# An audio tower on one core: who splits the weights, when batch 1's taps run, and where the last batches' second products and stores stand

## The chip, the cores and the metric

The kernel runs on one core of one Trainium2 chip. The metric is the device time of one execution in microseconds, lower is better. TensorE (PE) does the matmuls, VectorE (DVE), ScalarE (ACT) and GpSimd (POOL) the elementwise work, SyncE (SP) starts the transfers. The engines run side by side, each through its own list of instructions in order, and wait for each other by semaphores.

## What is computed

Eight batches of 750 frames with 192 features go through one block: a token front end (seven-tap convolution, pointwise product, relu, pooling by two, 2D Fourier transform, norm), an attention over tokens with 12 heads, and a routed feed-forward block. Cut to its steps:

```python
h = conv7_per_feature(x) + b_dw                       # "taps": 7 multiply-adds over 750 frames
h = maxpool2(relu(h @ w_pw + b_pw))                   # 375 tokens of 192
h = layernorm(real(fft2(h))) * gamma + beta           # first norm
w = layernorm(h) @ w_qkv                              # 12 heads of 64
Pi = softmax(sum_d (w / norm_n(w))**2 * temp)         # over the tokens
h = h - (w * Pi / (1 + Pi_norm @ w**2)) @ w_out + b_out
z = layernorm(h); n = layernorm(z) * g1 + b1          # routed block on z
s = sigmoid(n @ Wr + br)                              # the 56 lowest scores get attention
merged = where(lowest, softmax(q k / 4) v @ Wo + bo, (n + s * pooled) @ Wm + bm)
h2 = z + merged
n2 = layernorm(h2) * g2 + b2
out = h + h2 + gelu(n2 @ W1 + bf1) @ W2 + bf2
```

## The kernel before

Tokens lie on 125 partitions by 3 tiles where they are normed, and 192 features on 96 partitions by 2 where they are multiplied. Five weights (w_qkv, W1, Wk, Wv, Wm) are used in two parts: a high part (the weight rounded to fp32r) and a low part (the weight minus the high part), and the tokens likewise, so that a `split_product` is three matmuls.

`pipeline` runs ten steps on every engine: `step(p, q, r, w)`. In step k the front end and token attention of batch p = k run beside the routed block of batch q = k - 1, the feed-forward products of batch r = k - 2 and, on DVE, the taps of batch w = k + 1. Step 0 has only a front (and the taps of batch 1), steps 3 to 6 are a loop, step 8 has no front, and step 9 has only the feed-forward products of batch 7. The taps of batch 0 come ahead of step 0 in three tiles (`depthwise_first`, L376).

The order of each engine is written out by hand in its `step`:

- **POOL** (L776): clears whole tiles, splits w_qkv (L785 to L794: a copy, then a subtraction), then in step 0 the other four weights behind batch 0's norms. Beside that it takes the power of every norm and makes two additions a batch.
- **SP** (L286): loads, then x of batch 1 when batch 0's taps are done (L302), 22 transfers of weights (L306), then W1 into the space in which w_qkv lay (L309) once w_qkv is split; one store a batch (L319).
- **DVE** (L697): in step 0 pools batch 0, then the first norm (L414 on), the token split (L452), taps 0 to 2 of batch 1, head sums (L458 to L464), taps 3 and 4, the maximum of the token logits (L469), the token softmax and products, taps 5 and 6, and the third norm.
- **ACT** (L981): relu, the spectrum's copies (L853 on), sines, token split (L869), squares, exponentials, gelus.
- **PE** (L1318): `forward_up` (L1292) is the first product of the feed-forward block with W1, 6 blocks of 128 columns; `forward_down` (L1306) the second with W2, 3 tiles by 6 blocks, each two matmul instructions. In step 8 the second products of batch 6 stand between the attention steps of batch 7: tile 0 ahead of the last `turn` (a transpose of probabilities), tile 1 in two halves behind `values`, tile 2 in two parts around the output products (`mixed`, `replaced`, L1284). In step 9 all first products stand ahead of all second ones. `forward_down` waits for all six gelus once.

Behind the output products DVE adds them up and norms (`fifth_norm`, `fifth_norm_end`), PE transposes the result n2 (L1046), ACT and DVE split it, and the next first product can start. `result` (L694) adds the second products to the residual in two pieces, and SP stores the batch. The first product writes the same PSUM tile yb as the second, so it waits for the results of the batch before (L1299).

Of the kernel before, what the change touches and what calls it, by code (L numbers as in the profile page):

```python
# [4 lines left out]
B, S, D, K = 8, 750, 192, 7  # L5
# [29 lines left out]
def audio_tower(nc, dram, out):  # L35
# [3 lines left out]
    with ExitStack() as ctx:  # L39
# [112 lines left out]
        w_qkv32 = probsT[0:C].rearrange("c j t q -> c (j t q)")[:, 0:CT * IT * 128].rearrange("c (t i) -> c t i", t=CT)  # L152
        n2 = sb("n2", [P, T, D])
# [23 lines left out]
        split = signal("split")  # L177
# [73 lines left out]
        MEMSETS, WEIGHTS = 5, 5  # L251
        SPLIT = MEMSETS + 2 * WEIGHTS
# [9 lines left out]


# [18 lines left out]
        def first(b):  # L282
            return isinstance(b, int) and b == 0

        @block.sync
        def _(sp):  # L286
# [21 lines left out]
            sp.wait_ge(split.sem, MEMSETS + 2)  # L308
# [20 lines left out]
            for b in range(B - 3, B):  # L329
                store(b)  # L330
            sp.wait_ge(*stored.of(B - 1))

        @block.vector
        def _(dve):
# [41 lines left out]
            def depthwise_first():  # L376

                dve.wait_ge(*x_ready.of(0))
                for t in range(T):
# [3 lines left out]
                    for k in range(K):  # L383
                        for c in range(CT):
# [7 lines left out]
                            ins.then_inc(sem, 1)  # L392

# [295 lines left out]
            def result(b, i):  # L689
# [4 lines left out]
                dve.tensor_tensor(y_out[:, t0:t1, :], yb[0:P, i, 0:D * (t1 - t0)].rearrange("p (t d) -> p t d", d=D),  # L694
                                  res_f[:, t0:t1, :], ALU.add).then_inc(y_done.sem, 1)

            def step(p, q, r, w):  # L697
# [63 lines left out]
                if last:  # L761
                    result(r, 0)
                    result(r, 1)
# [3 lines left out]
                if middle:  # L767
                    forward_input(q)
                if front:
# [6 lines left out]
        def _(pool):  # L776
            pool.memset(half3[:], -0.5).then_inc(consts.sem, 1)
            pool.memset(xhT[:].bitcast(fp32), 0.0).then_inc(split.sem, 1)
            pool.memset(n2T[:].bitcast(fp32), 0.0).then_inc(split.sem, 1)
            pool.memset(nT[:].bitcast(fp32), 0.0).then_inc(split.sem, 1)  # L780
            pool.memset(w_v[:].bitcast(fp32), 0.0).then_inc(split.sem, 1)
            pool.wait_ge(split.sem, 4)
            pool.memset(nT[C:C + 1, 0, 0, :].bitcast(fp32), 1.0).then_inc(split.sem, 1)

            def split_weight(k, parts, weight):  # L785

                high, low = (parts[:, i, ..., 0:weight.shape[-1]] if len(weight.shape) == 3 else parts[:, i] for i in range(2))
                pool.tensor_copy(high, weight).then_inc(split.sem, 1)
                pool.wait_ge(split.sem, MEMSETS + 2 * k + 1)
                pool.tensor_tensor(low, weight, high, ALU.subtract).then_inc(split.sem, 1)  # L790

            pool.wait_ge(consts.sem, FILLS)
            pool.wait_ge(qkv_in.sem, QKV)
            split_weight(0, w_qkv, w_qkv32)  # L794
# [6 lines left out]
            def step(p, q, r, w):  # L801
# [10 lines left out]
                if first(p):  # L812
                    pool.wait_ge(rest_in.sem, REST)
                    pool.wait_ge(w_1_in.sem, 16)
                    split_weight(1, w_1, w_qkv32)
                    split_weight(2, w_k, w_k32)
                    split_weight(3, w_v, w_v32)
                    split_weight(4, w_mp, w_m[:])
# [20 lines left out]
        def _(act):  # L839
# [7 lines left out]

            def spectrum_parts(b):
# [13 lines left out]
            def front_input(b):  # L862
                act.wait_ge(*xhT_ready.of(b))
                if first(b):
                    act.wait_ge(split.sem, MEMSETS)
# [27 lines left out]
            def routed_input(b):  # L893
# [3 lines left out]
                else:  # L897
                    act.wait_ge(split.sem, SPLIT)
# [46 lines left out]
            def exponentials(b, j):  # L945
                act.wait_ge(*qmax_done.of(b, j + 1))
                if j == 0 and first(b):
                    act.wait_ge(split.sem, SPLIT)
# [18 lines left out]
            def forward_input(b):  # L967
                act.wait_ge(*n2T_ready.of(b))
                if first(b):
                    act.wait_ge(split.sem, MEMSETS)  # L970
# [515 lines left out]
```

## Time and profile before

| | |
|---|---|
| three timed runs | 654.84, 647.49, 654.38 us; median 654.38 |
| the profiled execution | 647.86 us |
| its span, first to last instruction | 646.0 us |
| mean granted PE clock over the span | 0.917 of full speed |
| busy share of the span | PE 85%, weight loads 70%, DVE 70%, ACT 36%, POOL 15% |
| chain that ended last, by engine | PE 58%, DVE 23%, ACT 11%, waiting to issue 6% |
| steps 2 to 7 | about 66.5 us each, PE clock at full |

Times in the rows are microseconds from the start of the span. An engine's busy time counts its own instructions, and a transfer's time runs from issue to landing. In the chain of waits each piece is followed back to what released it. A granted clock of 1.00 is 2.4 GHz, 0.50 is 1.2 GHz; where the profile has no record of it, as in the first 33 us, it shows 1.00.

### The profile page before, as it was taken

The numbers are of one execution on the slowest core, as the hardware profiler recorded it, in microseconds if no ns is written. First come the engines' busy times: TensorE is split into PE (matmuls) and PEld (weight loads), VectorE is DVE, ScalarE is ACT, GpSimd is POOL, SyncE is SP. The second block draws the span as 40 slices with busy tenths as digits, with TensorE's granted clock in tenths as the row PEclk, the third lists the DMA queues.
The fourth block names the chain that finished last, engine by engine and source line by source line (L and its number), as shares of the span: only waits on it lengthen the run. The fifth ranks groups of instructions, "written<-read, shape, count | busy, mean of one in ns | idle before, by whom it ended". The sixth has DMA issues, their size and how long they took to land.

```text
span 646.0 us, 9489 instructions
## 1 busy us (share of the span) xinstructions
PE 547.0 (85%) x3344; PEld 449.4 (70%) x3344; DVE 450.1 (70%) x1234; ACT 231.0 (36%) x614; POOL 94.4 (15%) x76
## 2 busy tenths in 40 slices
PE   1447398979999999999999999999989998787976
PEld 1326176758777878777877787788768777775765
DVE  5738868576878887789778887788778564824130
ACT  0014113440357035712581158125721564124311
POOL 5318010100210021002100301030103010200010
PEclk9987589576999999999999999999999999959689
DMA  8240010010000000010001000100000000000000
GB/s 209 75 124 1 0 36 2 1 36 1 1 1 24 15 19 1 2 36 18 0 0 36 18 0 0 36 18 0 0 0 19 2 0 1 19 0 2 1 18 18
DMA packets 8212, 12.73 MB, mean 20 GB/s; under 512 B 1891, under 2 KB 6717, under 8 KB 8184
## 3 DMA queue, kind: packets, MB, share of 16 engines
q1 hardware_dynamic: 8184, 12.37, 7.2%
q8 instruction: 16, 0.26, 0.2%
q14 instruction: 12, 0.10, 0.1%
HBM read 10.07 MB, written 2.30 MB: 19 GB/s over the span
## 4 chain that ended last, share of the span: by engine, by line
PE 58%; DVE 23%; ACT 11%; issue 6%; DMA 1%; POOL 1%; DVEq 0%; ACTq 0%; SPq 0%
PE xb L1138 8%; PE yb L1054 8%; PE zb L1054 7%; PE yb L1314 7%; PE xb L1084 5%; ACT probs L952 3%; PE xb L1093 3%; ACT w_sq L879 2%; DVE dw L390 2%; DVE nr L541 2%; PE zb L1284 2%; ACT w_s L878 2%; DVE st L343 2%; PE zb L1211 2%; ACT probsT L957 2%
## 5 line engine op out<-in xcount | busy, mean ns | idle before, releaser
L799 POOL TENSOR_TENSOR rs<-ve,half 125x3 f32<-125x3 f32 (+1 forms) x32 | 33.6, 1049 | 510.2 <-DVE ve L355 442.3
L372 DVE SCALAR_TENSOR_TENSOR dw<-x_in,w_dw_sb,dw 96x750 f32<-96x750 f32 x84 | 81.0, 1013 | 0.2
L1054 PE MATMUL yb<-n2T,w_sb 96*128 96x376 f32 x288 | 63.3, 366 | 5.5 <-DVE n2T L687 5.0
L1054 PE MATMUL xb<-xhT,w_qkv_sb 96*128 96x376 f32 x288 | 63.7, 367 | 4.8 <-DVE xhT L452 3.4
L1314 PE MATMUL yb<-w_sb,gelu 128*125 128x192 f32 x288 | 57.4, 344 | 6.3 <-ACT probs L952 5.7
L1054 PEld LDWEIGHTS xb<-xhT,w_qkv_sb 96*128 96x128 f32 x288 | 52.4, 205 | 11.3 <-DVE xhT L452 6.8
L1054 PEld LDWEIGHTS yb<-n2T,w_sb 96*128 96x128 f32 x288 | 52.8, 205 | 8.2 <-DVE n2T L687 5.5
L1314 PEld LDWEIGHTS yb<-w_sb,gelu 128*125 128x125 f32 x288 | 47.7, 193 | 12.7 <-ACT probs L952 7.1
L1138 PE MATMUL xb<-scratch,w_sq 128*125 128x192 f32 x288 | 52.7, 346 | 4.1 <-ACT scratch L890 4.1
L1138 PEld LDWEIGHTS xb<-scratch,w_sq 128*125 128x125 f32 x288 | 51.3, 202 | 4.9 <-DVE scratch L514 4.5
L957 ACT ACTIVATE probsT<-zb 125x384 f32<-125x384 f32 x48 | 26.5, 552 | 27.5 <-PE zb L1248 27.5
L1084 PE MATMUL xb<-dft_n_sb,pooled_h 125*96 125x376 f32 x96 | 33.6, 502 | 0.9 <-DVE pooled_h L401 0.9
L492 DVE TENSOR_TENSOR w_sq<-w_s,xb 128x376 f32<-128x376 f32 x48 | 25.2, 538 | 10.9 <-PE xb L1130 10.9
L979 ACT ACTIVATE gelu<-yb,b_sb 128x375 f32<-128x375 f32 x48 | 26.7, 571 | 14.8 <-PE yb L1054 13.4
L1248 PEld LDWEIGHTS zb<-ident_sb,probs 128*125 128x125 f32 x144 | 23.0, 206 | 12.9 <-issue 10.6
L1074 PE MATMUL xb<-w_pw_sb,dw 97*125 97x192 f32 x64 | 17.9, 364 | 15.1 <-DVE dw L390 14.6
L1130 PE MATMUL xb<-pi_parts,head_sel_sb 128*128 128x376 f32 x48 | 19.0, 452 | 13.7 <-DVE pi_parts L485 12.9
L890 ACT ACTIVATE scratch<-w_out_sb,natt 128x192 f32<-128x192 f32 x24 | 9.2, 445 | 58.3 <-DVE natt L512 58.3
L1248 PE MATMUL zb<-ident_sb,probs 128*125 128x128 f32 x144 | 28.2, 310 | 2.0 <-ACT probs L952 2.0
L973 ACT ACTIVATE n2T<-zb 96x750 fp32r<-96x750 f32 x8 | 6.3, 792 | 63.4 <-PE zb L1046 63.4
L878 ACT ACTIVATE w_s<-xb 128x375 f32<-128x375 f32 x48 | 25.5, 531 | 6.0 <-PE xb L1054 5.7
L1084 PEld LDWEIGHTS xb<-dft_n_sb,pooled_h 125*96 125x96 f32 x96 | 15.6, 170 | 15.8 <-issue 14.4
(186 smaller groups left out, 1142.8 us busy)
## 6 DMA issues: line engine op xcount, KB each, us to landing
x_in<-in_x SPq DMA_DIRECT2D x8, 567.0 KB, 4.3
out<-res_f SPq DMA_DIRECT2D x8, 281.2 KB
probsT<-in_w_qkv SPq DMA_DIRECT2D x1, 576.0 KB, 7.0
w_out_sb<-in_w_out SPq DMA_DIRECT2D x1, 576.0 KB
w_sb<-in_w SPq DMA_DIRECT2D x1, 576.0 KB
probsT<-in_w SPq DMA_DIRECT2D x1, 576.0 KB, 4.5
rows_sb<-in_rows SPq DMA_DIRECT2D x1, 504.0 KB
dft_n_sb<-in_dft_n SPq DMA_DIRECT2D x1, 493.5 KB
```

Source lines behind the costliest of these rows:

```text
L372: ins = dve.scalar_tensor_tensor(out=dw[0:C, c, :], in0=src, scalar=w_dw[:, c, k:k + 1], in1=dw[0:C, c, :], op0=ALU.mult, op1=ALU.add)
L492: dve.tensor_tensor(u[:, j, :], w_s[:, j, :], xb[:, j % 2, 0:NE], ALU.mult).then_inc(u_done.sem, 1)
L799: pool.tensor_tensor(out_[:], in_[:], half3[:] if len(in_.shape) == 3 else half3[:, 0, :], ALU.pow).then_inc(rs.sem, 1)
L878: act.activation(w_s[:, j, 0:N], xb[:, j % 2, 0:N], ACT.Copy)
L952: act.activation(probs[:, j, 0:N], score_bank(j)[:, 0:N], ACT.Exp, bias=nmax[:, j:j + 1], accum_out=psum_p[:, j:j + 1]).then_inc(prob_done ...
L957: act.activation(probsT[:, j, :, :], zb[0:P, 2 + j % 2, 0:T * 128].rearrange("p (t q) -> p t q", q=128), ACT.Copy).then_inc(prT_done.sem, 1)
L979: act.activation(gelu[:, j, 0:N], yb[:, j % 2, 0:N], ACT.Gelu, bias=b_1[:, j:j + 1]).then_inc(gelu_done.sem, 1)
L1054: ins = mm(o, a[:, k], b[:, l], start=start and k + l == 0, stop=stop and k == 1)
L1084: ins = mm(xb[0:C, c, 0:2 * KF], pooled_h[:, t, chan(c)], dft_n[:, t, :], start=(t == 0), stop=(t == T - 1))
L1138: ins = mm(o, u[:, j, tok(t)], w_oa[:, j, :], start=(j == 0), stop=(j == IT - 1))
L1248: ins = pe.transpose(zb[0:P, 2 + j % 2, 128 * t:128 * t + 128], probs[:, j, tok(t)], ident[:])
L1314: ins = mm(o, gelu[:, j, tok(t)], w_2[:, j, :], start=(j == 0), stop=(j == IT - 1))
```

## The change

The five weights are split by ACT (high part, `split_high`) and DVE (low part, `split_low`); POOL splits nothing, and clears only the padding of the tiles. In step 0 ACT splits w_qkv behind relu, and Wk, Wv, Wm and W1, in this order, behind the sines. DVE subtracts w_qkv behind the pooling, and the other four behind the token split. SP waits for the first subtraction ahead of its W1 load. Batch 1's taps 0 to 3 move ahead of the first norm of batch 0, taps 4, 5 and 6 to the squares; none are left ahead of the maximum and at the step's end.

In step 8 the second products of batch 6 leave the attention: tiles 0 and 1 stand behind the last output product and ahead of the transposes of n2, tile 2 behind them. Of the two results the second moves behind DVE's part of the split of n2. In step 9 a block's second products (all three tiles) follow the first products of the block two later; they write the tile zb. In every batch the second products of tile 0 wait for each gelu by itself. The last batch is stored in two parts, the first two tiles and the third.

```diff
@@ sync
-            sp.wait_ge(split.sem, MEMSETS + 2)
+            sp.wait_ge(lows.sem, 1)
             sp.dma_start(w_qkv32, dram["w_1"]).then_inc(w_1_in.sem, 16)
...
-            for b in range(B - 3, B):
+            for b in range(B - 3, B - 1):
                 store(b)
-            sp.wait_ge(*stored.of(B - 1))
+            for k, (t0, t1) in enumerate(((0, 2), (2, 3))):
+                sp.wait_ge(*y_done.of(B - 1, k + 1))
+                sp.dma_start(out[B - 1].rearrange("(t p) d -> p t d", p=P)[:, t0:t1], y_out[:, t0:t1, :]).then_inc(stored.sem, 16)
+            sp.wait_ge(stored.sem, 16 * B + 16)
@@ vector
+            def split_low(k):
+                weight, high, low = split_parts(k)
+                dve.wait_ge(highs.sem, 1 if k == 0 else WEIGHTS)
+                dve.tensor_tensor(low, weight, high, ALU.subtract).then_inc(lows.sem, 1)
...
-                taps = ((0, 0), (0, 2), (2, 3), (3, 3), (3, 5), (5, 7)) if first(p) else ((0, 3), (3, 4), (4, 5), (5, 6), (6, 7), (7, 7))
+                taps = ((0, 4), (4, 5), (5, 6), (6, 7), (7, 7), (7, 7)) if first(p) else ((0, 3), (3, 4), (4, 5), (5, 6), (6, 7), (7, 7))
                 if front:
                     pool_pairs(p)
+                if first(p):
+                    split_low(0)
...
                 if front:
                     front_input(p)
+                if first(p):
+                    for k in range(1, WEIGHTS):
+                        split_low(k)
...
                 if last:
                     result(r, 0)
+                if last and (front or not middle):
                     result(r, 1)
...
                 if middle:
                     forward_input(q)
+                if last and middle and not front:
+                    result(r, 1)
@@ gpsimd
-            pool.memset(xhT[:].bitcast(fp32), 0.0).then_inc(split.sem, 1)
...
-            pool.wait_ge(qkv_in.sem, QKV)
-            split_weight(0, w_qkv, w_qkv32)
+            for tokens in (xhT, n2T, nT):
+                pool.memset(tokens[:, :, :, N:NE].bitcast(fp32), 0.0).then_inc(pads.sem, 1)
...
-                    split_weight(1, w_1, w_qkv32)
...
-                    split_weight(4, w_mp, w_m[:])
@@ scalar
+            def split_high(k):
+                weight, high, _ = split_parts(k)
+                act.activation(high, weight, ACT.Copy).then_inc(highs.sem, 1)
...
                 if front:
                     relu(p)
+                if first(p):
+                    act.wait_ge(qkv_in.sem, QKV)
+                    split_high(0)
...
                 if front:
                     spectrum_sines(p)
+                if first(p):
+                    act.wait_ge(rest_in.sem, REST)
+                    for k in range(2, WEIGHTS):
+                        split_high(k)
+                    act.wait_ge(w_1_in.sem, 16)
+                    split_high(1)
@@ tensor
             def forward_down(b, t, j, q=None):
-                if t + j == 0:
-                    if q is not None:
+                if t == 0:
+                    if j == 0 and q is not None:
                         pe.wait_ge(*prob_done.of(q))
-                    pe.wait_ge(*gelu_done.of(b))
...
+                    pe.wait_ge(*gelu_done.of(b, j + 1))
-                o = yb[0:P, t // 2, D * (t % 2):D * (t % 2) + D]
+                o = zb[0:P, t, 0:D] if ends(b) else yb[0:P, t // 2, D * (t % 2):D * (t % 2) + D]
...
+            def last_forward(b):
+                for j in range(IT + 2):
+                    if j < IT:
+                        forward_up(b, j)
+                    if j >= 2:
+                        for t in range(T):
+                            forward_down(b, t, j - 2)
...
+                if last and not front:
+                    for t in range(2):
+                        for j in range(IT):
+                            forward_down(r, t, j, q)
                 if middle:
                     forward_input(q)
+                if last and not front:
+                    for j in range(IT):
+                        forward_down(r, 2, j)
```

## Rows read from the trace of the kernel before

**Rows 1.** Timeline, step 0's first half: start, duration, engine, line, count, idle before.
```profile
6.72 0.72 DVE L387 TENSOR_SCALAR dw<-x_in,w_dw_sb 96x250 f32<-96x250 f32 x2 [5.64 <-DMA x_in<-in_x]
...
17.35 5.05 DVE L387 TENSOR_SCALAR dw<-x_in,w_dw_sb 96x250 f32<-96x250 f32 x2
...
18.84 3.42 POOL L790 TENSOR_TENSOR w_qkv_sb<-probsT,w_qkv_sb 96x1536 fp32r<-96x1536 f32 x1
...
27.11 0.32 SPq L302 DMA_DIRECT2D x_in<-in_x  x1
...
36.41 0.48 ACT L853 ACTIVATE scratch<-xb 96x376 f32<-96x376 f32 x1 [5.98 <-PE xb L1084]
...
37.04 0.32 SPq L309 DMA_DIRECT2D probsT<-in_w  x1
...
41.05 0.46 DVE L414 TENSOR_TENSOR res<-xb,even 125x291 f32<-125x291 f32 x1 [10.23 <-PE xb L1093]
...
DMA to landing us min/median/max: 4.1/4.3/5.0
```

**Rows 2.** Timeline, step 0's second half and the start of step 1.
```profile
51.05 1.00 DVE L452 TENSOR_TENSOR xhT<-xb,xhT 96x375 fp32r<-96x375 f32 x2 [2.15 <-ACT xhT L869]
...
61.93 0.20 ACT L879 ACTIVATION_READ_ACCUMULATOR w_sq<-xb 128x1 f32 x1
...
63.15 0.16 DVE L460 TENSOR_SCALAR nrm<-nrm 128x6 f32<-128x6 f32 x1
...
63.98 2.22 PE L1119 MATMUL xb<-w_sq,rhead 128*32 128x375 f32 x12 [2.83 <-DVE rhead L464]
...
64.31 3.72 DVE L372 SCALAR_TENSOR_TENSOR dw<-x_in,w_dw_sb,dw 96x750 f32<-96x750 f32 x4
...
67.95 0.54 DVE L469 TENSOR_REDUCE lgm<-xb 128x1 f32<-128x375 f32 x1
...
96.69 1.24 DVE L369 TENSOR_SCALAR dw<-x_in,w_dw_sb 96x750 f32<-96x750 f32 x2
```

**Rows 3.** Groups by line: count | busy us, mean ns of one | idle before, releaser.
```profile
L687 DVE TENSOR_TENSOR n2T<-zb,n2T 96x750 fp32r<-96x750 f32 x8 | 7.4, 928 | 1.0 <-ACT n2T L973 1.0
...
L973 ACT ACTIVATE n2T<-zb 96x750 fp32r<-96x750 f32 x8 | 6.3, 792 | 63.4 <-PE zb L1046 63.4
```

**Rows 4.** Chain of waits, 580 to 646: start, duration, engine, tile, line, count.
```profile
603.80 3.89 PE yb L1314 x12
...
608.81 1.17 PE yb L1314 x6
...
614.38 0.85 PE yb L1314 x4
...
616.57 0.53 PE zb L1284 x2
...
621.73 0.86 PE zb L1046 x6
...
624.42 9.51 PE yb L1054 x36
...
634.58 6.13 PE yb L1314 x36
```

**Rows 5.** Windows: length, busy us of PE, PEld, DVE, ACT, POOL, clock, DMA share, GB/s.
```profile
140.00:153.30 13.30, 13.12 (x57) 9.92 (x58) 8.93 (x28) 1.51 (x4) 0.00 (x0) 0.50 0.00 0
...
607.20:617.20 10.00, 10.00 (x90) 8.19 (x88) 0.98 (x3) 0.85 (x2) 0.00 (x0) 1.00 0.01 2
...
624.40:631.10 6.70, 6.68 (x21) 6.68 (x22) 0.00 (x0) 2.02 (x4) 1.42 (x1) 0.50 0.09 28
...
642.00:645.20 3.20, 0.00 (x0) 0.00 (x0) 0.00 (x0) 0.00 (x0) 0.00 (x0) 0.94 0.31 88
```

**Rows 6.** Timeline of PE in a step of the loop: the pointwise product.
```profile
296.81 0.49 PE L1075 MATMUL xb<-w_pw_sb,dw 96*125 96x192 f32 x2
297.13 0.49 PE L1074 MATMUL zb<-w_pw_sb,dw 97*125 97x192 f32 x2
```

More of the change, by code:

```diff
@@ L250, in audio_tower, with split_parts @@
             (nsT[C:C + 1, 0, :], "ones_q"), (cxT[C:C + 1, 0, :], "ones_q2")) for x in pieces(dst, name)]
-        MEMSETS, WEIGHTS = 5, 5
-        SPLIT = MEMSETS + 2 * WEIGHTS
+        PADS, WEIGHTS = 6, 5
         FILLS, SELECTORS = 5, 6
         FIRST, DFT, NORM, QKV, HEAD, REST = (16 * len(x) for x in (firsts, dfts, norms, qkvs, heads, rests))
+        def split_parts(k):
+            weight, parts = ((w_qkv32, w_qkv), (w_1_32, w_1), (w_k32, w_k), (w_v32, w_v), (w_m[:], w_mp))[k]
+            return weight, parts[:, 0, :, 0:weight.shape[-1]], parts[:, 1, :, 0:weight.shape[-1]]
         def pipeline(eng, step):
@@ L283, in first, with ends @@
             return isinstance(b, int) and b == 0
+        def ends(b):
+            return isinstance(b, int) and b == B - 1
         @block.sync
@@ L777, in _ @@
             pool.memset(half3[:], -0.5).then_inc(consts.sem, 1)
-            pool.memset(xhT[:].bitcast(fp32), 0.0).then_inc(split.sem, 1)
[L779 to L792, printed above, removed]
-            pool.wait_ge(qkv_in.sem, QKV)
-            split_weight(0, w_qkv, w_qkv32)
+            for tokens in (xhT, n2T, nT):
+                pool.memset(tokens[:, :, :, N:NE].bitcast(fp32), 0.0).then_inc(pads.sem, 1)
+            pool.memset(w_v[:, :, :, D + 1:DV].bitcast(fp32), 0.0).then_inc(pads.sem, 1)
+            pool.wait_ge(pads.sem, 4)
+            pool.memset(nT[C:C + 1, 0, 0, 0:N].bitcast(fp32), 1.0).then_inc(pads.sem, 1)
+            pool.wait_ge(pads.sem, 5)
+            pool.memset(nT[C:C + 1, 1, 0, 0:N].bitcast(fp32), 0.0).then_inc(pads.sem, 1)
+            pool.wait_ge(pads.sem, PADS)
             def power(b, out_, in_, ve, rs):
@@ L1316, in forward_down @@
                     ins.then_inc(w2_ready.sem, 1)
+            def last_forward(b):
[5 more added lines that the diff above has]
+                            forward_down(b, t, j - 2)
             def step(p, q, r, w):
                 front, middle, last = p is not None, q is not None, r is not None
+                if not middle and not front:
+                    last_forward(r)
+                    return
                 if front:
@@ L1365, in step @@
                             turn(q, j - 1)
-                if last:
+                if last and front:
                     for j in range(IT):
@@ L1376, in step @@
                         values(q, c)
-                    if last:
+                    if last and front:
                         for j in range(3 * c, 3 * c + 3):
@@ L1392, in step @@
                     spread(p, 5)
-                if last:
+                if last and front:
                     forward_down(r, 2, 0)
@@ L1400, in step @@
                     replaced(q, 2)
-                if last:
+                if last and front:
                     for j in range(2, IT):
```

31 lines of the change are left out of this document (16 added, 15 removed).

## The prediction

> **What bounds the kernel now.** I read the page first: TensorE (PE) is busy most of the span, and its granted clock is full in the middle and drops at both ends. The middle, steps 2 to 7, is paced by PE, and the change leaves its order alone; so I read the two ends. First the timeline of the head [rows 1, 2]. The reader is to see that VectorE (DVE) sets the pace there: two TENSOR_SCALARs that take 0.72 us in the first tile take 5.05 us in the third, and the second of them ends just after GpSimd (POOL) has ended its 3.42 us subtraction at 22.26. Later DVE runs four batch-1 taps (3.72 us) while the logits that its next instruction needs are ready at 66.2 (63.98 + 2.22). Then the chain of waits of the last 45 us [rows 4]: in step 8 the second products of batch 6 (L1314) stand on the chain four times between batch 7's attention steps, and step 9 is first product, gelu, second product, one after another. Last the windows of the tail [rows 5], for the clock: PE has the full clock (1.00) from 607.2 to 617.2, half (0.50) from 624.4 to 631.1, and half at 603.8 too, where 12 second products take 3.89 us and 36 at full clock 6.13.
>
> **The head.** (a) Without POOL's subtraction the third tile's two instructions should take 0.72 us: 5.05 - 0.72 = 4.33 us, and everything behind them moves up, since PE, ScalarE (ACT) and DVE wait for that tile [rows 1].
> (b) What replaces it. ACT copies w_qkv (1536 elements a partition): from its 750-element copy at 0.79 us, an upper estimate of 1536/750 x 0.79 = 1.62 us. ACT's relu ended at 36.41 - 5.98 = 30.43, now 26.1; the copy ends at 27.7, and ACT was idle to 36.41, now 32.1. DVE subtracts: 1536/750 x 0.93 = 1.90 us, to 29.7 [rows 1, 3].
> (c) Batch 1's taps 0 to 3 follow: 1.24 us for the first pair, six more at 3.72/4 = 0.93 us, 6.8 us, to 36.5 [rows 2]. DVE was idle for 10.23 us to 41.05, which is now 36.7 [rows 1]: hidden, with 0.2 us to spare; without that cover every further microsecond would count. They need x of batch 1: issued at 27.11, now 22.8, landing after at most 5.0 us, 27.8 [rows 1].
> (d) The four other weights. SP sends w_1 behind x of batch 1 and the other weights, as before: at 37.04, now 32.7, when its wait for DVE's subtraction (29.7) is over. With 5.0 us to land that is 37.7. ACT's copies of all four are done by 37.7 + 1.62 + 3 x 0.4 = 40.5; they stand ahead of its split of batch 0's tokens, which DVE takes up at 51.05, now 46.7, so that they have 5 us to spare. DVE's four subtractions (1.90 + 3 x 0.5) and taps 4 to 6 (5.6 us) lie behind its own part of that split, which ends at 52.05, now 47.7; they end at 56.7; the squares that DVE waits for next end at 62.13 - 4.3 = 57.8 [rows 1 to 3]. Hidden, with 1 us to spare.
> (e) Before, DVE started on the squares' sums at 63.15 though they were ready at 62.13, because its mask product stood against POOL's last subtraction: 1.0 us gained. (f) The taps ahead of the logits' maximum are gone: 67.95 - 66.2 = 1.75 us. (g) Taps 5 and 6 at the step's end lay beside PE's output product: nothing.
> The smaller fills cost nothing and save nothing: they lay ahead of the first weight. Head: 4.33 + 1.0 + 1.75 = 7.1 us. Bounds: 0 if (c) or (d) comes late by as much, 8.5 with the clock's steps falling well.
>
> **Step 8.** Four runs of second products leave the chain between 603.8 and 617.1: 3.89 + 2 x 1.17 + 0.85 = 7.1 us, so 6.2 us of turns, values, context and output remain [rows 4]. These 6.2 us ran mostly at full clock, which PE had got back at 607.2, after the 12 second products at half clock (0.324 us each). Now those dense products are not there. I look for PE with this mix at half clock: from 140 to 153.3, in step 1, it was busy with it for 13.12 of 13.30 us, and the clock stayed at 0.50 [rows 5]. So I take half clock for the rest of the attention: 2 x 6.2 + 0.35 us for the DVE step that a second product covered = 12.8 us, to 616.6. Gain 0.5 us. The other bound is full clock from 607.2 on: the 3.4 us before that do 1.7 of the 6.2, and the end is at 607.2 + 4.5 + 0.35 = 612.05, 5.05 us gained.
> The Trainium skill (TensorE: Matmul & The Clock Gate, Part 1: The HAM clock gate) says that the slow state is the default and that sustained matmul work releases it. By that rule the stretch from 603.8, without a gap, would be released on its way, and the time would be that of the rival "full clock" below; the busy stretch just named speaks against it.
> Behind the attention DVE norms batch 7, from the last output product to n2: 621.7 - 617.1 = 4.6 us. PE now does 24 second products there: 24 x 0.17 (36 in 6.13) = 4.1 us at full clock, hidden; 24 x 0.324 = 7.8 us at half. Dense products got the clock back in 3.4 us (603.8 to 607.2) and 6.7 us (624.4 to 631.1); with 5 us it is 15 at half and 9 at full, 6.4 us, to 623.0, and the transposes, which stand behind them on PE, wait 1.8 us for nothing else. From the transposes to the first product it was 624.42 - 621.73 = 2.7 us; the last 12 second products (2.0 us) fit in there, but the second result now stands behind DVE's split, and the first product waits for it: 0.7 us more. First product at 626.4, 2.0 us later than before.
>
> **Step 9.** Before: 624.42 to 640.71, 16.3 us, of which 6.7 at half clock. Now PE comes in warm and gelu is covered by second products: 36 first products at 6.68/21/2 = 0.16 us, 5.7 us, and 36 second at 0.17, 6.1 us: 11.85 us, to 638.25 [rows 4, 5]. Gain, with the 2.0 us paid, 2.45 us. The first result now becomes ready only two matmuls ahead of the second, so about 0.2 us are added behind the last matmul.
> Two stores: the last store moved its bytes from 642.0 to 645.2 at a DMA share of 0.31, 5 of the 16 engines [rows 5]. If the second, a third of the bytes, uses other engines, the end comes 1.25 us sooner; if it queues behind the first on the same five, 0.15 us. I take 0.15, since one store leaves eleven engines free and nothing here shows that a store chooses them.
> The Trainium skill (DMA: Bandwidth & Descriptors, Why a DMA increments its semaphore by 16 and not by 1) says that such a transfer takes the largest count up to 16 that divides its rows, for 125 rows 5, and always the lowest-numbered. By it the sum has 0.15, by free choice 1.25. The share of 0.31 agrees on the five; no run here shows which five.
>
> **The sum.** 7.1 + 2.45 - 0.2 + 0.15 = 9.5 us. The profiled execution took 647.86 us, a span of 646.0 and 1.9 around it: 638.4 us. The runs shown lie at 647.49, 654.38 and 654.84, so this execution is the faster kind, 6.5 us under the median. I forecast on its footing; on the median's it would be 644.9.
>
> **Rivals.** *Full clock in the attention tail.* If PE does not lose the full clock in step 8, or has it back by 607, the products behind the attention are hidden: n2 at 612.05 + 4.6 = 616.65, first product 2.7 + 0.7 us later at 620.05, last matmul at 631.9, 8.8 us before 640.71: 632.0 us in all. For it: PE is busy without a gap. Against it: the stretch of step 1 in rows 5. A return between gives 634 to 637.
> *Half clock to the end of step 8.* All 36 at 0.324: the 24 end at 624.4, transposes (0.86), 12 more (3.9) and the second result put the first product at 629.5 and the last matmul at 641.4; the tail loses 0.7 us: 641.5.
> *The taps delay the first norm.* 0.2 us of cover in (c): if batch 1's x lands after 29.7, or ACT's copy or DVE's subtraction is longer, each microsecond is lost once. 4 us late gives 642.5. Against it: the latest landing of eight was 5.0 us.
> *The new waits cost, and the kernel is slower.* Each of the six second products of a batch's first tile now waits for its own gelu, 5 waits more in 7 steps, 35. At 0.27 us each they eat the 9.5 us; at 0.64 each the kernel is 13 us slower, 661. In the loop a matmul behind a wait that has long been met (297.13, the third frame) started 0.32 us after the one ahead, the pace of the rest: 0 [rows 6]. That speaks against it.
> *The split doesn't help.* DVE could stall for another reason in the third tile: then (a) falls and the time is 642.7. The end of POOL's subtraction within 0.2 us of DVE's speaks against it.
>
> **How the numbers follow.** Forecast 0.52; full clock or an early return 0.26; half to the end of step 8 0.06; late taps or no help from the split 0.12; waits 0.04. The time is the forecast's, 638.4. The low end is full clock with a microsecond to spare, 631; the high end is the forecast on the higher runs' footing and some late taps, 647. A change under 2% can't be told from none here: 2% under the median shown is 641.3. The forecast falls on either side of it by the footing, so its 0.52 is 0.2 faster and 0.32 same. Full clock: 0.25 and 0.01. Half: same. Late taps: 0.03 and 0.09. Waits: 0.01 same, 0.03 slower. Faster 0.48, same 0.49, slower 0.03.
>
> **What would show it.** Head: the third tile's L387 pair at 0.72 us, the first norm near 36.7, token maximum 7 us earlier. Tail: the granted clock between 604 and 617 decides; then when the transposes of n2 start after its last DVE step, and whether step 9 starts at full clock. I am wrong if the first norm waits for taps, if PE has gaps between the loop's second products, or if the clock drops in steps 0 and 1 at other places than before.

## The result and the profile after

The changed kernel takes 630.55 us (median of four: 629.41, 630.36, 630.74, 635.21) where the kernel before took 653.31 in the same measurement: a ratio of 0.971, with an interval of 0.967 to 0.975. Measured once more, beside the last experiment, it was 631.17 us and 0.970 (0.964 to 0.975). The forecast of 638.4 us had the direction, though its chances stood at 0.48 for faster and 0.49 for the same; it was 8 us too high, and the result lies half a microsecond under the low end of its range, 631. The rival "full clock in the attention tail", at 632.0, came within 1.5 us.

The profiled execution took 630.36 us, a span of 628.5 against 646.0. An execution's time depends on where in it TensorE (PE) falls to half clock, which differs between executions of one program, so medians here are over all executions and ratios over those within about 1.5% of each kernel's fastest. Where the 17.5 us of these two spans come from:

| stage | before | after | gain |
|---|---|---|---|
| start to step 1 | 88.90 | 82.73 | 6.17 |
| step 1 | 72.57 | 69.36 | 3.21 |
| steps 2 to 7, to the last output product of step 7 | 398.72 | 398.72 | 0 |
| step 8, from there to DVE's part of the split of n2 | 63.24 | 58.57 | 4.67 |
| from there to the first product of step 9 | 0.99 | 1.63 | -0.64 |
| step 9, first product to last | 16.27 | 12.28 | 3.99 |
| last product to the end | 5.29 | 5.17 | 0.12 |

Timeline of the changed kernel, step 0 on DVE and ACT: start, duration, engine, line, operation, tiles, count, idle before.

```profile
17.42 0.72 DVE L398 TENSOR_SCALAR dw<-x_in,w_dw_sb 96x250 f32<-96x250 f32 x2
...
26.06 1.47 ACT L859 ACTIVATE w_qkv_sb<-probsT 96x1536 fp32r<-96x1536 f32 x1
...
27.56 1.75 DVE L408 TENSOR_TENSOR w_qkv_sb<-probsT,w_qkv_sb 96x1536 fp32r<-96x1536 f32 x1 [1.01 <-ACT w_qkv_sb L859]
29.24 1.24 DVE L380 TENSOR_SCALAR dw<-x_in,w_dw_sb 96x750 f32<-96x750 f32 x2
...
38.02 0.46 DVE L430 TENSOR_TENSOR res<-xb,even 125x291 f32<-125x291 f32 x1 [2.08 <-PE xb L1117]
...
52.02 5.54 DVE L383 SCALAR_TENSOR_TENSOR dw<-x_in,w_dw_sb,dw 96x750 f32<-96x750 f32 x6
...
59.30 0.17 DVE L476 TENSOR_SCALAR nrm<-nrm 128x6 f32<-128x6 f32 x1 [1.47 <-ACT w_sq L892]
...
61.65 0.55 DVE L485 TENSOR_REDUCE lgm<-xb 128x1 f32<-128x375 f32 x1 [1.09 <-PE xb L1144]
```

The third tile's pair takes 0.72 us, where it took 5.05 [rows 1]. (In the kernel before the first of the two ended just behind POOL's copy of w_qkv, at 18.9, and the second just behind its subtraction; both are gone.) DVE now waits for PE ahead of the first norm (2.08 us) and of the token maximum (1.09 us), and for ACT's squares ahead of 59.30; before, the maximum followed the taps without a wait [rows 2].

Windows of step 1, step 8, a part of its attention, step 9 and the last store of the changed kernel: length, busy us of PE, PEld, DVE, ACT, POOL, granted clock, DMA share, GB/s.

```profile
82.70:152.10 69.40, 59.21 (x347) 47.71 (x347) 51.79 (x148) 22.30 (x66) 6.97 (x6) 0.85 0.03 9
550.80:609.40 58.60, 46.86 (x264) 37.19 (x262) 23.81 (x71) 19.19 (x45) 5.18 (x4) 0.77 0.01 4
587.70:597.70 10.00, 9.12 (x57) 6.62 (x60) 2.00 (x5) 5.24 (x16) 0.00 (x0) 0.50 0.00 0
611.00:623.30 12.30, 12.28 (x72) 12.00 (x72) 0.22 (x1) 4.27 (x7) 1.44 (x1) 1.00 0.08 23
...
624.50:627.70 3.20, 0.00 (x0) 0.00 (x0) 0.00 (x0) 0.00 (x0) 0.00 (x0) 1.00 0.30 88
```

The same three stages of the kernel before:

```profile
88.90:161.50 72.60, 64.56 (x347) 51.67 (x347) 52.24 (x148) 22.33 (x66) 6.99 (x6) 0.76 0.03 9
...
560.20:623.40 63.20, 49.52 (x268) 39.16 (x266) 24.01 (x71) 19.22 (x45) 5.19 (x4) 0.76 0.02 4
624.40:640.70 16.30, 15.61 (x72) 15.00 (x72) 0.56 (x1) 3.74 (x7) 1.42 (x1) 0.79 0.04 11
```

Step 1 has the same instructions in both and differs in the clock, 0.85 against 0.76. Step 8 is shorter at nearly the same clock, step 9 has the full clock throughout.

Chain of waits of the changed kernel, end of step 8 and step 9: start, duration, engine, tile, line, count.

```profile
603.18 0.83 DVE h L681 x2
...
606.54 1.09 DVE n L697 x3
...
607.67 0.84 PE zb L1070 x6
608.52 1.97 PE yb L1340 x12
610.51 0.37 DVE res_f L711
...
611.01 3.35 PE yb L1078 x18
614.36 0.98 PE zb L1340 x6
...
620.37 2.62 PE zb L1340 x16
```

Second products (L1340) are gone from the attention. The 24 of tiles 0 and 1 aren't on the chain: DVE's norm (603.18 to 607.63) is, and the transposes (L1070) start at its end. Tile 2's twelve and the second result (L711) are on it, ahead of the first product at 611.01.

### The profile page after: what moved, and what is told of

Same layout as the page of the kernel before. It is cut to its first block, busy times and chain, and to the rows that moved or that the text cites. A ratio compares the mean times of both kernels' runs of the same rounds, so it can differ in the third digit from the quotient of the medians.

```text
span 628.5 us, 9490 instructions
## 1 busy us (share of the span) xinstructions
PE 537.3 (85%) x3344; PEld 441.9 (70%) x3344; DVE 444.2 (71%) x1239; ACT 234.6 (37%) x619; POOL 68.4 (11%) x67
## 4 chain that ended last, share of the span: by engine, by line
PE 58%; DVE 21%; ACT 12%; issue 6%; DMA 1%; POOL 1%; DVEq 0%; ACTq 0%; SPq 0%; POOLq 0%
PE xb L1163 8%; PE yb L1078 7%; PE zb L1078 7%; PE xb L1108 5%; PE yb L1340 5%; ACT probs L967 3%; PE xb L1117 3%; ACT w_sq L892 2%; PE xb L1078 2%; DVE dw L401 2%; DVE nr L557 2%; ACT w_s L891 2%; DVE w_sq L508 2%; PE xb L1144 2%; DVE junk L516 2%
## 5 line engine op out<-in xcount | busy, mean ns | idle before, releaser
L383 DVE SCALAR_TENSOR_TENSOR dw<-x_in,w_dw_sb,dw 96x750 f32<-96x750 f32 x84 | 79.0, 990 | 0.2
L1078 PE MATMUL yb<-n2T,w_sb 96*128 96x376 f32 x288 | 60.2, 350 | 4.2 <-DVE n2T L703 3.2
L1078 PEld LDWEIGHTS yb<-n2T,w_sb 96*128 96x128 f32 x288 | 49.1, 191 | 6.9 <-DVE n2T L703 4.2
L1340 PE MATMUL yb<-w_sb,gelu 128*125 128x192 f32 x252 | 48.7, 336 | 5.3 <-ACT probs L967 5.3
L1340 PEld LDWEIGHTS yb<-w_sb,gelu 128*125 128x125 f32 x252 | 40.3, 187 | 10.5 <-ACT probs L967 6.5
L1108 PEld LDWEIGHTS xb<-dft_n_sb,pooled_h 125*96 125x96 f32 x96 | 15.9, 172 | 16.3 <-issue 14.9
```

Source lines behind the costliest of these rows:

```text
L383: ins = dve.scalar_tensor_tensor(out=dw[0:C, c, :], in0=src, scalar=w_dw[:, c, k:k + 1], in1=dw[0:C, c, :], op0=ALU.mult, op1=ALU.add)
L1078: ins = mm(o, a[:, k], b[:, l], start=start and k + l == 0, stop=stop and k == 1)
L1108: ins = mm(xb[0:C, c, 0:2 * KF], pooled_h[:, t, chan(c)], dft_n[:, t, :], start=(t == 0), stop=(t == T - 1))
L1340: ins = mm(o, gelu[:, j, tok(t)], w_2[:, j, :], start=(j == 0), stop=(j == IT - 1))
```

## The experiments

**The head alone.** The changed kernel with the second products of step 8, step 9 and the last store as before:

```diff
-                if not middle and not front:
-                    last_forward(r)
-                    return
...
-                if last and front:
+                if last:
                     for j in range(IT):
                         forward_down(r, 0, j, q)
...
-                if last and not front:
-                    for t in range(2):
-                        for j in range(IT):
-                            forward_down(r, t, j, q)
```

> The head alone: the split by ScalarE and VectorE and batch 1's taps as in the changed kernel; second products, step 9 and the last store as before. Theory (the head works through the third tile of the depthwise product and through the taps): step 1 starts 6.2 us earlier than before, at 82.7, and the stretch of step 1 from its token maximum to its output product gains another 3.2 us, since it starts from the same state as in the changed kernel; the time falls by 6 to 9.4 us, ratio 0.986 to 0.991. Rival (the 3.2 us of step 1 are chance, not a consequence of the head): step 1 starts 6.2 us earlier and step 2 as well. Rival (the gain is the tail's alone): less than 3 us.

Four executions between 638.16 and 648.21 us, median 644.51, where the kernel before had 652.05. In the trace step 1 starts at 81.6, 7.3 us earlier (0.7 of it because step 0's first matmul started at 11.5 in place of 12.3), and then takes as long as before:

```profile
81.60:154.20 72.60, 64.57 (x347) 51.67 (x347) 52.24 (x148) 22.33 (x66) 6.97 (x6) 0.76 0.03 9
```

So the head is worth about what was forecast, and the 3.2 us of step 1 do not belong to it: the rival held.

**The tail alone.** The kernel before with steps 8 and 9 and the two stores of the change, head as before; against the changed kernel:

```diff
-                taps = ((0, 4), (4, 5), (5, 6), (6, 7), (7, 7), (7, 7)) if first(p) else ...
+                taps = ((0, 0), (0, 2), (2, 3), (3, 3), (3, 5), (5, 7)) if first(p) else ...
...
+                    split_weight(1, w_1, w_qkv32)
+                    split_weight(2, w_k, w_k32)
+                    split_weight(3, w_v, w_v32)
+                    split_weight(4, w_mp, w_m[:])
```

> The tail alone: late second products in step 8, products between the gelus in step 9 and two last stores on the kernel before; the head as before. Theory (second products out of the attention's way, and a TensorE without gaps in step 9 that keeps the full clock): steps 0 to 7 as before, the split of n2 in step 8 comes 4.7 us earlier and step 9 takes 12.0 us in place of 16.3; 8 us faster, ratio 0.988. Rival (the full clock in the changed kernel's step 8 came from the head, which shifted where the clock falls): step 8's attention runs at half clock to its end as the forecast had it, the split of n2 is no earlier than before, and only step 9's part is gained: 2.5 us, ratio 0.996.

642.29 us, ratio 0.988 (0.983 to 0.992). Step 1 is 3.2 us shorter here although its head is that of before, step 8 and step 9 are as in the changed kernel:

```profile
89.40:158.70 69.30, 59.14 (x346) 47.62 (x346) 51.69 (x148) 22.33 (x66) 6.99 (x6) 0.85 0.03 9
557.50:616.10 58.60, 47.82 (x263) 37.87 (x262) 23.81 (x71) 19.22 (x45) 5.17 (x4) 0.74 0.02 4
617.70:630.00 12.30, 12.26 (x72) 11.96 (x72) 0.26 (x1) 4.26 (x7) 1.45 (x1) 1.00 0.08 23
```

The tail's gain is its own and doesn't need the head. Over all traces without additional matmuls in step 1 it took 68.8 to 74.7 us with the old head or a part of the new one and 69.4 to 72.6 with the whole new one, 69.4 or less where its clock was 0.85 and 72.5 or more where it was 0.76 or 0.77: its 3.2 us are chance and not an effect of the change.

**The split with the old places of the taps.**

```diff
-                taps = ((0, 4), (4, 5), (5, 6), (6, 7), (7, 7), (7, 7)) if first(p) else ...
+                taps = ((0, 0), (0, 2), (2, 3), (3, 3), (3, 5), (5, 7)) if first(p) else ...
```

> The head with the split by ScalarE and VectorE, but batch 1's taps at their places of before; the tail as before. Theory: the third tile's pair of instructions takes 0.72 us (5.05 before), the first norm starts 3 us earlier, the four later subtractions (3.4 us) and two taps lie ahead of the squares, two taps (1.86 us) delay the token maximum again: step 1 starts 4 us earlier than before, ratio 0.993. Rival (the taps are what gained): step 1 starts within 1 us of before. Rival (the taps' places are worth nothing): 6.2 us earlier, as with the new places.

649.58 us, ratio 0.991 (0.986 to 0.996). Timeline on DVE:

```profile
16.67 0.72 DVE L395 TENSOR_SCALAR dw<-x_in,w_dw_sb 96x250 f32<-96x250 f32 x2
...
36.38 0.46 DVE L427 TENSOR_TENSOR res<-xb,even 125x291 f32<-125x291 f32 x1 [7.80 <-PE xb L1111]
...
58.81 3.72 DVE L380 SCALAR_TENSOR_TENSOR dw<-x_in,w_dw_sb,dw 96x750 f32<-96x750 f32 x4
62.45 0.53 DVE L482 TENSOR_REDUCE lgm<-xb 128x1 f32<-128x375 f32 x1
```

The same maximum in the run with the head alone:

```profile
60.57 0.55 DVE L482 TENSOR_REDUCE lgm<-xb 128x1 f32<-128x375 f32 x1 [1.09 <-PE xb L1138]
```

The pair is at 0.72 us, and the maximum, which again follows taps, comes 5.5 us earlier than before. With the new places it came 7.4 us earlier (head alone): 1.9 us for the taps, about as priced (1.75). Little of that lasts to the end of step 0. Step 1 starts at 82.3 here and at 81.6 with the head alone, because PE's product at the end of step 0 took 7.62 us here and 8.81 there; the clock came back 3.2 us after its start here and 5.6 us there. So step 1 starts 6.6 us earlier than before. My 4 us missed, and the rival that the taps' places are worth nothing (6.2) came nearest. The first norm gained 4.7 us, not 3. The split is nearly the whole gain of the head.

**The taps alone**, on the kernel before, GpSimd (POOL) splitting:

```diff
-                taps = ((0, 0), (0, 2), (2, 3), (3, 3), (3, 5), (5, 7)) if first(p) else ...
+                taps = ((0, 4), (4, 5), (5, 6), (6, 7), (7, 7), (7, 7)) if first(p) else ...
```

> Batch 1's taps at their new places alone; the five weights split by GpSimd as before, the tail as before. Theory: the third tile's pair stays at 5.05 us and the first norm at 41; the token maximum no longer waits for taps, 1.75 us earlier, and with it step 1: ratio 0.997. Rival (the taps collide with GpSimd's later subtractions, so that the taps themselves run longer): no gain or a loss up to 3 us, and single taps of over 0.93 us show it.

656.11 us, ratio 0.996 (0.989 to 1.002): no difference that can be told. The maximum came at 67.61, only 0.34 us earlier. The rival's collision is in the trace. Timeline of POOL, then of DVE:

```profile
52.02 3.47 POOL L790 TENSOR_TENSOR w_sb<-probsT,w_sb 96x1536 fp32r<-96x1536 f32 x1
```

```profile
52.06 4.22 DVE L372 SCALAR_TENSOR_TENSOR dw<-x_in,w_dw_sb,dw 96x750 f32<-96x750 f32 x1
...
52.06 10.96 DVE L372 SCALAR_TENSOR_TENSOR dw<-x_in,w_dw_sb,dw 96x750 f32<-96x750 f32 x6
```

The first tap starts 0.04 us after POOL's subtraction of w_1 has started and takes 4.22 us in place of 0.93; the six take 10.96 where the changed kernel's take 5.54. The Trainium skill (SBUF — State Buffer, Who interferes with whom) says that VectorE and GpSimd share one pair of ports as an exclusive lock, which an instruction of VectorE with two inputs from SBUF needs against one of GpSimd that reads SBUF. This trace agrees. So the two halves of the head depend on each other: the taps can stand there because POOL is silent.

**Step 8's late second products alone**, on the kernel before.

```diff
-                if last:
+                if last and (front or not middle):
                     for j in range(IT):
                         forward_down(r, 0, j, q)
...
+                if last and middle and not front:
+                    for t in range(2):
+                        for j in range(IT):
+                            forward_down(r, t, j, q)
                 if middle:
                     forward_input(q)
+                if last and middle and not front:
+                    for j in range(IT):
+                        forward_down(r, 2, j)
```

> The kernel before with only step 8's second products moved behind the attention (tiles 0 and 1 ahead of the transposes of n2, tile 2 behind them, the second result behind the split of n2); head, step 9 and the last store as before. Theory (the attention loses 7.1 us of foreign products, which then lie beside VectorE's norm): step 8, from its start to the split of n2, is shorter by 4.7 us or more; step 9 as before at 16.3 us; 4 us faster, ratio 0.994. Rival (the forecast's step: without those dense products TensorE stays at half clock to the end of the attention): the 24 products are not hidden, the first product of step 9 comes 2 us later, ratio 1.003.

Nine executions from 637 to 656 us and one of 749.04 whose cause wasn't seen, median 648.36 where the kernel before had 650.98. The ratio of 0.985 (0.980 to 0.990) is that of the five up to 646 us alone. The profiled one took 651.30 us, and in it step 8 is at half clock nearly throughout, the case of the forecast. Windows of step 8, its half clock and step 9, then the timeline of PE and DVE:

```profile
557.30:629.20 71.90, 61.77 (x263) 48.79 (x262) 23.92 (x70) 19.21 (x45) 5.18 (x4) 0.55 0.01 4
560.30:625.00 64.70, 56.96 (x229) 44.26 (x230) 19.34 (x53) 17.64 (x43) 4.04 (x4) 0.50 0.00 1
630.90:644.10 13.20, 12.53 (x72) 11.92 (x72) 0.56 (x1) 4.24 (x7) 1.45 (x1) 1.00 0.07 22
```

```profile
622.16 5.58 PE L1321 MATMUL yb<-w_sb,gelu 128*125 128x192 f32 x24
627.58 0.81 PE L1053 MATMUL zb<-ident_sb,n 125*96 125x125 f32 x6
```

```profile
625.17 1.08 DVE L684 SCALAR_TENSOR_TENSOR n<-n,rs,rows_sb 125x192 f32<-125x192 f32 x3
```

Here the 24 products aren't hidden: DVE's n2 is done at 626.25 and the transposes start 1.3 us later (I had 1.8). Step 8 is 8.7 us longer than in the profile before, and step 9, which starts at full clock, 13.2 us in place of the 16.3 that I expected. So the forecast's mechanism exists; how often it comes isn't shown. Up to 580.6 this trace and that of the tail alone agree: the clock fell at 560.2 in both, and from there PE was busy for 16.1 of 20.4 us in both. There it came back at 580.6, here only at 625.1. What decides between the two isn't shown by any run.

**Step 9's order alone**, on the kernel before, its second products in zb:

```diff
+                if not middle and not front:
+                    last_forward(r)
+                    return
```

> The kernel before with only step 9 changed: a block's second products follow the first products of the block two later; head, step 8 and the last store as before. Theory (the products cover the gelus, and a TensorE without gaps gets the clock back sooner): step 9 takes 12 us when it starts at full clock and at most 16 when it starts at half; 2 to 4 us faster, ratio 0.994 to 0.997. Rival (step 9 gains only behind the new step 8, because with the old one it starts at half clock): less than 1 us.

649.50 us, ratio 1.000 (0.996 to 1.004). Step 9:

```profile
626.20:641.30 15.10, 15.07 (x72) 14.77 (x72) 0.23 (x1) 3.73 (x7) 1.44 (x1) 0.80 0.04 12
```

It took 15.1 us in place of 16.0 to 16.3: the order covers the gelus, worth about 1 us, but the clock is 0.80 as before. My theory missed here; the rival (only behind the new step 8) held.

**The last store by rows.**

```diff
-            for k, (t0, t1) in enumerate(((0, 2), (2, 3))):
-                sp.wait_ge(*y_done.of(B - 1, k + 1))
-                sp.dma_start(out[B - 1].rearrange("(t p) d -> p t d", p=P)[:, t0:t1], y_out[:, t0:t1, :]).then_inc(stored.sem, 16)
+            sp.wait_ge(*y_done.of(B - 1))
+            for p0, p1 in ((0, 112), (112, P)):
+                sp.dma_start(out[B - 1].rearrange("(t p) d -> p t d", p=P)[p0:p1], y_out[p0:p1]).then_inc(stored.sem, 16)
```

> The changed kernel with the last batch stored as rows 0 to 111 and rows 112 to 124 of all three tiles in place of two tiles and one. Theory (a store of 125 rows is carried by 5 of the 16 engines, one of 112 rows by 16): packets last 3.25 x 5 / 16 = 1.0 us in place of 3.25, and from the last matmul to the end of the span it is 3.3 us in place of 5.5. Rival (the store is bound by something else than the number of engines): 5.5 us and a DMA share of about 0.3 as before.

One execution, 627.90 us. From the last matmul to the end of the span it is 3.56 us, in the changed kernel 5.17; 3.3 were expected. The window of the store:

```profile
623.30:625.50 2.20, 0.00 (x0) 0.00 (x0) 0.00 (x0) 0.00 (x0) 0.00 (x0) 1.00 0.48 131
```

0.48 of 2.2 us and 0.30 of 3.2 us are the same engine time, about 1 us, spread over more engines. By the rule of the Trainium skill that the prediction weighed (DMA: Bandwidth & Descriptors, Why a DMA increments its semaphore by 16 and not by 1), 112 rows go to 16 engines and 125 to 5; the gain of 1.6 us agrees with it, and the two parts of the change, both of 125 rows, gained only 0.12 us.

**Additional matmuls in step 8.** The changed kernel, with products that nobody reads in PE's waits (13, 8, 8, 4, 2 and 6):

```diff
+            def warm(n, bank):
+                for _ in range(n):
+                    mm(bank[:, 0, 0:128], dft_n[:, 0, 0:128], dft_n[:, 1, 0:128], start=True, stop=True)
...
+                if middle and not front:
+                    pe.wait_ge(*h1_done.of(B - 1))
+                    warm(13, xb)
                 if last:
                     forward_up(r, 0)
```

> The changed kernel with 41 additional matmuls in step 8 whose products nobody reads, in six of TensorE's waits (13 ahead of the first feed-forward product, 8 ahead of batch 7's input, 8 ahead of keys and values, 4, 2 and 6 later). Theory (step 8's time is set by where the clock falls after TensorE's waits at its start): the clock stays at full from step 7 on through most of step 8, and the split of n2 comes 5 to 10 us sooner after step 8's start than the 58.1 us of the changed kernel; ratio to the kernel before 0.955 to 0.965 in place of 0.971. Rival (the clock falls for other reasons): the half-clock stretches stay, 27 us in step 8, and the additional matmuls cost up to 3 us.

625.31 us, ratio 0.961 (0.954 to 0.968). Step 8:

```profile
555.20:606.70 51.50, 47.49 (x345) 40.02 (x344) 23.81 (x71) 19.10 (x45) 5.19 (x4) 0.97 0.02 5
```

51.5 us in place of 58.6, at a clock of 0.97 in place of 0.77, with more work on PE. The clock is what step 8 lost this time to, and work in PE's waits keeps it; which of the six places matter was not tried one by one.

**The same in steps 0, 1 and 8**, with the store by rows. Two of the 22 places:

```diff
+                if first(p):
+                    warm(34, yb)
                 if front:
                     front_input(p)
...
+                if first(q):
+                    warm(10, yb)
                 if front:
                     token_logits(p)
```

> The changed kernel with the last batch stored as 112 and 13 rows, and with additional matmuls whose products nobody reads in TensorE's waits of step 0 (95), step 1 (36) and step 8 (41). Theory (steps 0, 1 and 8 lose time where the clock falls after TensorE's waits): from the first full clock on, near 31 us, hardly any stretch at half clock is left; steps 0 and 1 together are 5 to 12 us shorter than the 152 us of the changed kernel, step 8 takes 51.5 us to the split of n2, the store saves 1.6: 611 to 618 us, ratio 0.938 to 0.948. Rival (steps 0 and 1 are paced by VectorE and ScalarE, so that the clock there costs nothing and the additional matmuls delay): 620 us or more, ratio 0.952 or more.

607.58 us (606.11, 606.90, 608.26, and one of 640.63 whose cause wasn't seen), ratio 0.938 (0.928 to 0.948): better than both kernels. Steps 0, 1 and 8:

```profile
12.00:74.80 62.80, 54.54 (x347) 47.64 (x347) 47.46 (x116) 15.55 (x38) 3.16 (x3) 0.97 0.27 74
74.80:138.90 64.10, 62.05 (x419) 51.06 (x419) 51.67 (x148) 22.22 (x66) 6.98 (x6) 0.95 0.04 10
537.60:587.50 49.90, 45.89 (x346) 38.78 (x344) 23.79 (x70) 19.10 (x45) 5.19 (x4) 1.00 0.02 5
```

Step 2 starts at 138.9 in place of 152.1, 13 us gained, a little more than the 12 at the top of my expectation; the time, too, is under the 611 to 618 that I expected.

**The additional matmuls on the kernel before**, in step 8 alone, at the same six places.

> The kernel before with the same 41 additional matmuls in step 8 alone: everything of the change left out. Theory (step 8 has two separate costs, the clock and the second products on the attention's chain): at full clock the old order takes the 51.5 us of the changed kernel with the additional matmuls, plus 36 second products at 0.17 us, 6.1 us: 57.6 us to the split of n2, and step 9 starts at full clock and takes 13.2 us as in the run with the late second products alone; ratio 0.98 to 0.985. Rival (the clock's cost came from the order of the products): step 8 stays above 63 us; ratio over 0.993.

640.99 us, ratio 0.987 (0.982 to 0.993). Steps 8 and 9, then the norm of n2 and what follows it:

```profile
557.10:613.80 56.70, 49.81 (x351) 41.64 (x348) 24.02 (x71) 19.07 (x45) 5.19 (x4) 0.95 0.02 6
614.80:631.10 16.30, 15.60 (x72) 14.99 (x72) 0.56 (x1) 3.75 (x7) 1.44 (x1) 0.79 0.03 9
...
607.00:611.30 4.30, 1.69 (x10) 1.27 (x8) 4.08 (x16) 0.00 (x0) 0.96 (x1) 1.00 0.00 0
611.50:621.50 10.00, 8.15 (x27) 7.71 (x28) 1.61 (x3) 3.79 (x5) 1.44 (x1) 0.50 0.11 30
```

Step 8 is 56.7 us (57.6 expected): at nearly full clock the old order costs 5.2 us more than the new one. Step 9 missed my 13.2: the clock was at half from 611.4 to 621.6, from behind DVE's norm of n2, in which PE has little to do in the old order (1.69 of 4.30 us).

**That wait filled too**: 17 more additional matmuls beside the norm and 8 ahead of step 9, every product of the kernel at its old place.

```diff
+                if middle and not front:
+                    warm(17, xb)
                 if middle:
                     forward_input(q)
```

> The kernel before with the 41 additional matmuls in step 8 and 25 more: 17 behind the last output product, beside VectorE's norm of n2, and 8 ahead of the first product of step 9; their products are read by nobody. Every product of the kernel keeps its place of before. Theory (in the changed kernel step 9 is faster mainly because the late second products fill TensorE's wait for that norm, so that the clock no longer falls there): step 9 runs at full clock and takes 13.2 us in place of 16.3, and the median is about 3 us below that of the run without the 25. Rival (it is the order in step 9 that gains, by covering the gelus): step 9 stays at 16 us, or the clock falls all the same; the median is unchanged or higher.

638.58 us, ratio 0.980 (0.973 to 0.987); 2.4 us under the run without the 25. The two intervals overlap, so the trace has to carry the reading; in it step 9 alone is 3 us shorter:

```profile
619.50:632.70 13.20, 12.53 (x72) 11.97 (x72) 0.56 (x1) 3.72 (x7) 1.44 (x1) 1.00 0.03 10
```

13.2 us, as expected, in the old order. Of the 4 us that step 9 gained, 3 are the clock, which the late second products keep up beside the norm, and 1 the order.

**The changed kernel unaltered, for its spread.**

> The changed kernel unaltered, for the spread of its executions. Theory (the clock's state in steps 1 and 8 is chance, and when step 8 runs at half clock throughout, the late second products aren't hidden, as in the run with them alone): most executions between 627 and 636 us as in the four known, but some of 640 to 650. Rival (the new head and step 9 keep the changed kernel out of that case): none above 637.

629.58, 629.94, 630.11, 632.22, 634.49 and 645.74 us. One of six is above 640. It wasn't profiled; that it is the case of the half clock in step 8 is only argued (its mean clock was 0.897, against 0.935 in the fastest three). The profiled one is the 632.22. Its steps 1 and 8:

```profile
81.50:154.00 72.50, 64.49 (x346) 51.60 (x346) 52.14 (x148) 22.31 (x66) 6.97 (x6) 0.76 0.03 9
552.70:611.30 58.60, 47.83 (x264) 37.84 (x263) 23.77 (x70) 19.19 (x45) 5.18 (x4) 0.74 0.02 4
```

So one program, the changed kernel, took 69.4 us for step 1 in one profile and 72.5 in another, and 58.6 for step 8 in both.

## Why the prediction was right or wrong

**The head: right in the sum, not in every term.** 7.1 us were forecast; 6.2 in the pair of profiles, 6.5 over the traces (step 1 starts at 88.9 on average in the six with the whole head of before, 82.4 in the five with the whole new one and no additional matmuls in step 0). The pair at 0.72, the copy (1.47 for 1.62) and the subtraction (1.75 for 1.90) came as priced, and the taps ended at 35.9, ahead of the first norm. But the first norm came 3.0 us earlier, not 4.33, in the profiled pair: the transform that PE does ahead of it took 6.22 us for 5.41. More of it at half clock would explain that, but the profile has no record of the clock ahead of 31.2, and the other 0.5 us stay open. The 1.75 us of the taps show at the maximum (1.9), but only 0.7 us are left of them at the start of step 1 in the run with the taps at their old places, where PE's last product of the step got the clock back sooner. Late taps (the rival "the taps delay the first norm") did not occur.

**Step 1: not in the sum.** 3.2 of the 17.5 us of the pair of profiles are chance, as the head alone, the tail alone and the second profile of the changed kernel show. The prediction named it as a sign of being wrong if the clock dropped in steps 0 and 1 at other places than before. In step 1 it did: half clock from 136.2 to 156.7 before, and only from 133.6 to 137.0 and 143.8 to 147.2 in the changed kernel.

**Step 8: the term that was mis-sized.** I took half clock to the end of the attention, hence 0.5 us of gain and a first product 2.0 us late. The changed kernel had half clock only from 587.6 to 597.8 there, so that the attention ended 4.7 us sooner after step 8's start and the 24 products were hidden; the first product came 4.0 us sooner. My bound for full clock, 5.05 us, agrees with what the old and new orders differ by at nearly full clock (56.7 and 51.5 us: 5.2). I had also put the return of the clock at 607.2 down to the twelve dense second products ahead of it. In the profiles of the kernel before and of the head alone it came 47.0 and 47.1 us after the start of step 8; in four with the new order, without those products there, 47.0 to 47.2 us after it. So it can come as early without them. The evidence I chose, a stretch of step 1 that stayed at half clock with PE busy [rows 5], was real; so was the half-clock case (72 us, in the run with step 8 alone). What failed is the step from one stretch at half clock to the likeliest course of another: the new step 8 took 58.6 us in four traces and 72 in one. No program was profiled in both cases, so that it is chance within one program is argued from the spread of the executions. The half clock should have had a smaller chance than 0.52, and the full clock a larger one than 0.26.

**Step 9: right, for the reason only half seen.** 11.85 us forecast, 12.28 measured. "PE comes in warm" carried 3 us of it and the covered gelus 1; what keeps PE warm is that second products now fill the norm's wait, which stood in the prediction only as something hidden.

**The median.** I forecast on the footing of the profiled 647.86 us. Old steps 8 without additional matmuls took 63.2 (that profile), 63.9, 68.0, 69.9 and 70.8 us, new ones 58.6 in four of five traces, so the profile of before was a short one of its kind, and the medians differ by 21 to 23 us where the pair of spans differs by 17.5. That the rival's 632.0 lies so near the measured median is partly luck: it was added up on that short profile, its tail was worth 8.8 us where 8.0 were measured (4.67 - 0.64 + 3.99) and its head 7.1 for 6.2, and step 1's 3.2 us, which it did not have, made up for both.

**The stores and the waits: right.** Behind the last matmul the sum had a loss of 0.05 us (0.15 - 0.2), and 0.12 were gained; the DMA share of 0.30 over the store is again five engines, for both parts together. Steps 2 to 7 take the same time to a hundredth of a microsecond in the pair of profiles: the 35 waits cost nothing.

## What to carry to other kernels

Price each stage at both clocks, and ask of every wait of TensorE what the stage behind it will run at; moving work into such a wait pays twice, once for its old place and once for the clock. Where no useful work fits, matmuls whose products nobody reads did it here: 172 of them, with the store by rows, took 631 us to 608. Weights that GpSimd prepared beside VectorE's chain cost that chain 4.3 us here; ScalarE and VectorE prepared them in time in which they had waited.

## What the runs showed of the hardware that was not expected

- TensorE stayed at half clock for 64.7 us (560.3 to 625.0, step 8 alone) while it was busy for 57 of them; with additional matmuls in the waits the same step ran at 0.95 to 1.00 (in four traces).
- One VectorE tap took 4.22 us beside GpSimd's subtraction of 3.47 us, 0.93 without it.
- The same instructions of step 1 took 68.8 to 69.4 us at a clock of 0.85 and 72.5 to 74.7 at 0.76 or 0.77, in different traces; the changed kernel alone showed both.
- The same work led to two courses of the clock: after 20.4 us at half clock with PE busy for 16.1 of them it came back at 580.6 in one trace (tail alone) and stayed at half to 625.1 in another (step 8 alone).
- The last 0.29 MB went out at 88 GB/s over 3.2 us as 125 rows, and at a mean of 131 GB/s over 2.2 us as 112 rows and 13.
